# Row maxima handed over in four transfers of two adjacent partitions instead of two transfers of four scattered ones

## What is computed

```python
x = x + 0.5 * ffn(layernorm(x))          # 7 routed experts (top 2) and one shared, hidden size 352
def attn(x):                             # x = layernorm(x); 16 heads of 8 features, 1,024 tokens
    v = (x @ w_v + v_b) ...
    q = (x @ w_q + q_b) @ w_k.T + k_b
    kh = x.reshape(b, s, H, D).transpose(0, 2, 1, 3)
    scores = einsum('bhqd,bhkd->bhqk', qh, kh) / sqrt(D)
    scores = where(causal, scores, finfo.min)
    probs = softmax(scores, axis=-1)
    return einsum('bhqk,bhkd->bhqd', probs, v) ... @ c_proj_w + c_proj_b
x = x + attn(layernorm(x))
x = x + 0.5 * ffn(layernorm(x))
```

## Time and profile before

| | us |
|---|---|
| median of 3 runs | 605.41 |
| lowest, highest | 604.32, 606.02 |
| profiled execution, its time | 604.32 |
| profiled execution, its span | 602.4 |
| PE busy (share) | 555.1 (92%) |
| DVE busy | 456.9 (76%) |
| ACT busy | 328.7 (55%) |
| POOL busy | 255.8 (42%) |

### The profile page before, as it was taken

How to read it: one execution, slowest core, us unless ns; L and a number is a source line. 1 busy time by engine, 2 the same in 40 slices (tenths; PEclk the granted TensorE clock), 3 DMA queues, 4 the chain that set the end, 5 groups by cost and what they waited for, 6 DMA issues and landing times.

```text
span 602.4 us, 11848 instructions
## 1 busy us (share of the span) xinstructions
PE 555.1 (92%) x3738; PEld 425.0 (71%) x3738; DVE 456.9 (76%) x1151; ACT 328.7 (55%) x701; POOL 255.8 (42%) x400
## 2 busy tenths in 40 slices
PE   1988999998885889999999999999999899999995
PEld 1878999997773545656565656565654889999995
DVE  3678777778559997878787878787555778777875
ACT  4454444457525435757575757577677434444633
POOL 7398956445243421212121212111135878864440
PEclk9999999999997979999999999999999989999998
DMA  9911436932581462504031313120000121341314
GB/s 255 303 47 52 111 94 150 243 114 75 158 240 54 158 142 71 157 8 152 16 130 37 132 34 122 47 96 0 3 2 19 32 74 53 89 117 36 114 52 112
DMA packets 46888, 58.74 MB, mean 97 GB/s; under 512 B 6183, under 2 KB 37678, under 8 KB 46062
## 3 DMA queue, kind: packets, MB, share of 16 engines
q1 hardware_dynamic: 38160, 46.77, 27.7%
q0 software_dynamic: 4480, 9.25, 4.8%
q10 hardware_dynamic: 4190, 1.98, 1.3%
HBM read 38.09 MB, written 28.00 MB: 110 GB/s over the span
## 4 chain that ended last, share of the span: by engine, by line
PE 73%; DVE 12%; POOL 4%; issue 4%; DMA 3%; ACT 3%; SPq 0%; DVEq 0%; POOLq 0%; ACTq 0%
PE psum L1577 12%; PE psum L1620 12%; PE psum L1642 11%; PE psum L848 5%; PE psum L850 4%; PE psum L849 4%; PE psum L866 4%; PE psum L884 4%; PE psum L887 3%; DVE mxp L1724 2%; POOL z_rows L1114 2%; PE psum L1580 2%; PE psum L907 1%; PE psum L1605 1%; POOL idle L1124 1%
## 5 line engine op out<-in xcount | busy, mean ns | idle before, releaser
L1781 ACT ACTIVATE probs<-psum 128x512 f32<-128x512 f32 (+1 forms) x304 | 155.0, 580 | 90.8 <-PE psum L1620 72.5
L1724 DVE TENSOR_REDUCE mxp<-psum 128x1 f32<-128x512 f32 (+3 forms) x304 | 182.6, 656 | 24.9 <-PE psum L1577 20.9
L1577 PE MATMUL psum<-keys,queries 128*128 128x512 f32 (+1 forms) x304 | 116.1, 440 | 4.9 <-DVE mxp L1724 3.7
L1832 POOL TENSOR_SCALAR_AFFINE_SELECT probs<-probs 128x512 f32<-128x512 f32 x64 | 40.8, 637 | 172.9 <-ACT probs L1781 172.9
L1137 POOL DMA_INDIRECT y_rows<-ys,to_row x76 | 74.5, 981 | 80.4 <-DVE ys L1045 52.7
L1620 PE MATMUL psum<-queries,keys 128*128 128x512 f32 (+3 forms) x384 | 106.0, 369 | 0.6 <-ACT probs L1781 0.3
L956 ACT ACTIVATE silu<-psum 128x352 f32<-128x352 f32 x107 | 49.7, 465 | 103.0 <-PE psum L850 102.4
L1001 DVE TENSOR_TENSOR act<-silu,psum 128x352 f32<-128x352 f32 x107 | 55.4, 518 | 46.5 <-ACT silu L956 45.7
L1577 PEld LDWEIGHTS psum<-keys,queries 128*128 128x128 f32 x304 | 56.3, 194 | 42.6 <-DVE mxp L1724 37.2
L1620 PEld LDWEIGHTS psum<-queries,keys 128*128 128x128 f32 x384 | 66.0, 190 | 24.6 <-issue 9.4
L1642 PE MATMUL psum<-probs,vg 128*32 128x512 f32 (+3 forms) x768 | 76.0, 494 | 0.3
(11 more groups left out here) (260 smaller groups left out, 1014.7 us busy)
## 6 DMA issues: line engine op xcount, KB each, us to landing
z_rows<-q_stack SPq DMA_DIRECT2D x12, 682.5 KB, 5.6
keys<-q_stack SPq DMA_DIRECT2D x12, 512.0 KB
keys<-k_stack SPq DMA_DIRECT2D x32, 128.0 KB, 6.0
queries<-q_stack SPq DMA_DIRECT2D x8, 512.0 KB, 5.7
zg_early<-z_rows SPq DMA_DIRECT2D x44, 65.0 KB, 1.9
yc<-y_rows SPq DMA_DIRECT2D x10, 256.0 KB, 3.9
zg_late<-z_rows SPq DMA_DIRECT2D x32, 65.0 KB
k_stack<-zt_h SPq DMA_DIRECT2D x8, 256.0 KB, 3.0
```

Of the source, the lines that this page charges most:

```text
L1577: ins = e.matmul(dst, K.queries[u][:, i * P:(i + 1) * P], K.keys[u][:, heads[0]:heads[-1] + 1, k0 * P:(k0 + nb) * P], start=True, stop=Tru ...
L1724: e.tensor_reduce(K.mxp[:, heads[0]:heads[-1] + 1, i, which], scores, AX.X, ALU.max).then_inc(K.A["taken"], 1)
L1781: e.activation(K.probs[:, kt % 2, heads[0]:heads[-1] + 1, q0:q1], src, ACT.Exp, scale=SCALE).then_inc(K.A["ex"], 1)
```

## The change

The layout of `mm_hl` goes from (part, head, tile) to (head, part, tile). The first transposition then yields both parts of heads 0 and 1, the second both parts of heads 2 and 3, where before the first yielded the high parts of all four heads and the second the low parts. `rows_load` issues one transfer for each head: 16 rows of `m_rows` go into two adjacent rows of `queries`. Before, it issued one for each part: 32 rows of `m_rows` into four rows of `queries` that stand 32 apart. The first two of the four wait for the first copy to `m_rows`, the other two for the second. All four add 16 to `ld_r`, so its counts go from 32 to 64.

```diff
-        K.mm_hl = sb("mm_hl", [P, 2, 4, KT], F32R, scope=s)
+        K.mm_hl = sb("mm_hl", [P, 4, 2, KT], F32R, scope=s)
...
     elif what == "mrow":
...
-                          K.mm_hl[:, n, :, :].bitcast(F32).rearrange("p j i -> p (j i)"), K.ident[:, :])
+                          K.mm_hl[:, 2 * n:2 * n + 2, :, :].bitcast(F32).rearrange("p j a i -> p (j a i)"), K.ident[:, :])
...
     if n == 0:
-        e.wait_ge(K.ld_r[v], 32 * loads(p, u, d))
+        e.wait_ge(K.ld_r[v], 64 * loads(p, u, d))
...
-            e.tensor_copy(K.mm_hl[:, 0, :, :], K.nmax[:, :, :]).then_inc(K.A["nm"], 1)
+            e.tensor_copy(K.mm_hl[:, 0:4, 0, :], K.nmax[:, :, :]).then_inc(K.A["nm"], 1)
...
-            e.tensor_tensor(K.mm_hl[:, 1, :, :], K.nmax[:, :, :], K.mm_hl[:, 0, :, :].bitcast(F32),
+            e.tensor_tensor(K.mm_hl[:, 0:4, 1, :], K.nmax[:, :, :], K.mm_hl[:, 0:4, 0, :].bitcast(F32),
...
-            e.wait_ge(K.ld_r[(u + d - 1) % 3], 32 * loads(p, u, d - 1))
+            e.wait_ge(K.ld_r[(u + d - 1) % 3], 64 * loads(p, u, d - 1))
...
-    for part in range(2):
-        e.wait_ge(K.A["taken"], r + part + 1)
-        dst = K.queries[v][part:part + 97:32, :].bitcast(F32).rearrange("j (i q) -> j i q", q=P)
-        src = K.m_rows[4 * KT * part:4 * KT * (part + 1), :].bitcast(F32)
-        e.dma_start(dst, src).then_inc(K.ld_r[v], 16)
+    for j in range(4):
+        if j % 2 == 0:
+            e.wait_ge(K.A["taken"], r + (j // 2 + 1))
+        dst = K.queries[v][32 * j:32 * j + 2, :].bitcast(F32).rearrange("p (i q) -> p i q", q=P)
+        e.dma_start(dst, K.m_rows[2 * KT * j:2 * KT * (j + 1), :].bitcast(F32)).then_inc(K.ld_r[v], 16)
```

## The result

The changed kernel takes 612.27 us at the median (610.32 to 616.05), the kernel before 605.32 in the same runs. The ratio is 1.012, with a 95% interval of 1.009 to 1.015, that is 5.2 to 9.2 us more. The forecast was 612.3. The ratios further down are to the kernel before as it was timed beside the experiment.

A forecast was written before the change was run, and what follows sets the result against it. PE was taken to bound the kernel, busy for 92% of the span. 5.9 us in the loop plus 1.0 in the prologue made 6.9 us, against the median of 605.41 a forecast of 612.3 us, range 608.0 to 614.8.

The forecast's parts named there:

- What bounds: Attention loop: PE is busy for all 30.00 us of a 30 us window, and DVE and ACT cannot work off a stall.
- The slack of 0.3 us: Loop bodies: the transfers could come 0.3 us later for free, as products of key tiles 5 and 6 hold unit 1.0.
- The price of an issue: SP's queue, line 1914: each issue takes 0.64 us with the gap, so four put the last landing 1.28 us later.
- The landing: Wait of line 1617: ends 1.9 us after the last transfer's issue, however many transfers went before.
- The loop: Six loop bodies: 1.28 us less 0.3 of slack is 0.98 us of waiting each, 5.9 us in all.
- `LAST_BUT_ONE`: Body `LAST_BUT_ONE`: the last landing, 1.28 us later at 432.2, stays hidden with 0.4 us to spare.
- The prologue: Prologue: no slack, unit 0.0 comes 1.28 us late; 1.0 us counted, since some slow-clock matmul work moves to full clock.
- the 1.20 us of the subtraction: DVE's subtraction in the prologue: counted as zero change, but its 1.20 us may be an outlier, bound 1.0 us below.
- The cheap issue: Rival, SP's queue: an issue period of 0.37 us costs 1.4 us in all, 606.8 us, not slower; 8% chance.
- The clock's fall: Rival, loop: each 1 us stall of PE halves its clock for some 7 us, about 20 us more, 632 us; 4%.

## Why the prediction was right

**What bounds.** Right. PE's idle time ahead of line 1620 grew from 0.6 to 7.9 us, 7.4 of it in front of these transfers, and DVE and ACT did not work it off: by the page DVE's idle time ahead of line 1724 went from 24.9 to 33.0 us, ACT's ahead of line 1781 from 90.8 to 97.7.

**The slack of 0.3 us.** Right in kind and a little too small. Three issues in the old form took SP 0.55 us longer than the two of before (1.78 against 1.23) and left a stall of 0.20; four took 1.03 longer (2.26) and left 0.66; the changed kernel's took 1.50 longer (2.73) and left 1.10. Each gives a slack of 0.35 to 0.4. The prediction had taken 0.1 off for the way from wait to load.

**The price of an issue.** The term that was mis-sized most. It was taken as 0.64 us with the gap from the transfers of before. In the changed kernel 2.73 us go by for four, 0.71 from the first to the next on the average (310.83 to 312.95 is 2.12 for three). The last landing came 1.5 us later and not 1.28 (4.1 us behind the first issue, where it was 2.6), and the stall was 1.1 and not 0.98: the slack that was taken too small hid part of that error. That the old price was near the new one was partly luck: 16 rows instead of 32 made it cheaper (0.50), neighbouring rows dearer (0.61).

**The landing.** Right: 1.88 us from the last issue (rows 4 and 5 gave 1.9) though two more went before. In the other forms it is 1.76 to 1.81, with three and with seven issues ahead of it.

**The loop.** 6.6 us from mark to mark against 5.9. The first body stalls 0.94 us, the others 1.07 to 1.10, `LAST_BUT_ONE` not at all, as said: its wait ends at 440.2, now with the last landing, and its weights are loaded at 440.49, so 0.3 us are left to spare.

**The prologue.** 1.0 us was predicted. The first pair of profiles shows 0.2 and the second 0.5, though PE stands still for 0.97 us there. The runs with four transfers in the prologue alone say 0.9 with an interval from -0.3 to 2.1; these are of the cheaper form, with a stall of 0.6 us. So the size of this term stays open. The reason given, that slow-clock work moves to where the clock is full, is what one execution shows; that another can take 1.8 us more was not foreseen. The remark that the 1.20 us of the subtraction may be an outlier was wrong: it is 1.20 again.

```profile
213.07 1.20 DVE L1732 TENSOR_TENSOR mm_hl<-nmax,mm_hl 128x32 fp32r<-128x32 f32 x1
```

**The rivals.** The cheap issue fell: no issue of these transfers took under 0.495 us in any kernel. With it falls what the Trainium skill gives in DMA: Bandwidth & Descriptors, in the section on the anatomy of one DMA, some 50 ns for the dispatch, if one reads it as the price of a transfer on SP's queue; it is written of POOL's. The clock's fall did not come at 1.1 us and came at 3.7.

The mechanism was right, and the sum was near in part because its errors lay on both sides: the loop was 0.7 us above it, and the prologue, by the profiles, 0.5 to 0.8 below. That it met the median within 0.1 us is luck, with an interval of 5.2 to 9.2 us for the difference.

## What to carry to other kernels

A wait that costs nothing may have its release a few tenths of a microsecond ahead of the need. Compare when it ends with when its transfers are issued: where that distance was the same everywhere, as here, every issue added in front of it was paid as soon as the slack was used up. Transfers that one queue issues in a row are best counted and not weighed: here a transfer of 4 KB took the queue as long as one of 16 KB. Releasing them one ring unit earlier took the stall of the loop away for 0.08 us per body. Two units earlier cost 0.4, with or without the added transfers: an engine with idle time on the average can still wait when work is moved past it, so the move has to be priced too.

## What the hardware showed that was not expected

- An issue of these transfers on SP takes, at the median and without the gap, 0.59 us for 32 rows into four rows 32 apart, 0.50 for 16 rows into two rows 32 apart, 0.61 for 16 rows into two neighbours, and 0.63 for 8 rows into one.
- A stall of PE of 1.1 us in an otherwise full loop left the clock at 2.4 GHz in every body (1.00 in every window of the loop); one of 3.7 us was followed by a stretch at 1.2 GHz.
- In one kernel it was 31.86 us in one execution and 33.82 in another from the prologue's first transfer to that of the first body, with granted clocks of 0.72 and 0.57 over 12 us.
